# Two accumulating products of a mixer block joined in one PSUM bank, with the hand-written step tables that go with it

## What is computed

```python
x = x + _L0_conv_ref(_gn(x), w_qkv, w_o)            # attention, 12 heads of 16, over 1024 tokens
x = x + _L1_conv_ref(_gn(x), w1, b1, w2, b2, bias_w, bias_b)

# _L1_conv_ref(x, ...)
bias = x @ bias_w.T + bias_b                         # the linear path
xf = jnp.fft.rfftn(xb, axes=(1, 2), norm='ortho')    # over H and W, four blocks of 48 channels
r1, i1 = relu(complex product with w1, + b1)
r2, i2 = second product with w2, + b2
out = jnp.fft.irfftn(complex(r2, i2), s=(H, W), axes=(1, 2), norm='ortho')
return out + bias
```

## Time and profile before

| | |
|---|---|
| median of three runs | 1474.7 us (1470.56 to 1479.0) |
| the profiled execution's own time | 1474.24 us |
| its span on the core | 1472.4 us |
| PE busy | 1414.4 us (96% of the span) |
| DVE, ACT busy | 1156.4 us (79%), 1009.3 us (69%) |
| TensorE clock granted, mean | 0.986 of full speed |

### The profile page before, as it was taken

The page is one execution under the profiler, slowest core; times in us unless marked ns, Lnnn a source line. Parts: engine busy times, 40 slices in busy tenths (PEclk is TensorE's granted clock), DMA queues, the critical chain, the costliest instruction groups (busy, mean ns, idle before and its releaser), DMA issues.

```text
span 1472.4 us, 27421 instructions
## 1 busy us (share of the span) xinstructions
PE 1414.4 (96%) x9984; PEld 682.2 (46%) x9984; DVE 1156.4 (79%) x2155; ACT 1009.3 (69%) x2018; POOL 187.6 (13%) x277
## 2 busy tenths in 40 slices
PE   6999889999999999999999999998999999999978
PEld 4543334545444454544545444544545454434455
DVE  4888888987899879987799878986799878988041
ACT  1267777677767777677767777676776777677812
POOL 2000001030013000040011200040010400040000
PEclk9699999999999999999999999999999999999999
DMA  7400431242430533333430523324322324312213
GB/s 149 78 12 17 95 66 29 44 106 74 84 88 24 121 83 61 69 86 87 94 84 21 127 67 72 74 65 91 88 62 50 82 76 87 88 30 65 64 44 89
DMA packets 100606, 106.37 MB, mean 72 GB/s; under 512 B 24760, under 2 KB 77560, under 8 KB 100472
## 3 DMA queue, kind: packets, MB, share of 16 engines
q1 hardware_dynamic: 98616, 102.80, 30.6%
q10 hardware_dynamic: 1856, 1.82, 0.6%
HBM read 26.99 MB, written 6.67 MB: 23 GB/s over the span
## 4 chain that ended last, share of the span: by engine, by line
PE 85%; DVE 7%; DMA 3%; SPq 2%; issue 1%; ACT 1%; POOL 0%; ACTq 0%; POOLq 0%; DVEq 0%
PE o_acc L1313 24%; PE ring L1289 16%; PE scores L1251 16%; PE ring L1336 10%; DVE row_max L1049 5%; PE ring L1325 3%; PE ring L1449 2%; PE ring L1436 2%; PE ring L1442 2%; PE ring L1355 2%; PE ring L1347 1%; PE ring L1428 1%; DMA rows_b<-rows_a 1%; PE ring L1455 1%; SPq L667 1%
## 5 line engine op out<-in xcount | busy, mean ns | idle before, releaser
L1049 DVE TENSOR_REDUCE row_max<-ring 128x1 f32<-128x512 f32 x1536 | 973.9, 682 | 180.9 <-PE ring L1289 174.6
L938 ACT ACTIVATE probs<-scores 128x512 f32<-128x512 f32 x1536 | 829.0, 600 | 260.6 <-PE scores L1251 259.7
L1289 PE MATMUL ring<-k_stack,q_stack 48*128 48x512 f32 x1536 | 592.5, 463 | 26.2 <-DVE row_max L1049 16.5
L1251 PE MATMUL scores<-q_stack,k_stack 50*128 50x512 f32 x1536 | 594.8, 460 | 1.3 <-ACT probs L938 1.2
L1313 PE MATMUL o_acc<-probs,v_aug 128*18 128x512 f32 x3072 | 405.5, 600 | 2.4 <-ACT probs L938 1.2
L1251 PEld LDWEIGHTS scores<-q_stack,k_stack 50*128 50x128 f32 x1536 | 243.7, 185 | 314.1 <-ACT probs L938 300.2
L1289 PEld LDWEIGHTS ring<-k_stack,q_stack 48*128 48x128 f32 x1536 | 247.6, 187 | 147.4 <-DVE row_max L1049 95.7
L583 POOL TENSOR_TENSOR inv_all<-o_raw,inv_all 128x1024 f32<-128x1024 f32 x23 | 54.5, 2371 | 573.9 <-DMA inv_all<-inv_rows 573.9
L1313 PEld LDWEIGHTS o_acc<-probs,v_aug 128*18 128x18 f32 x3072 | 52.0, 96 | 122.7 <-issue 86.9
L1336 PE MATMUL ring<-xt,w_qk 64*128 64x256 f32 x540 | 67.9, 379 | 1.3 <-DVE xt L1088 1.3
L1336 PEld LDWEIGHTS ring<-xt,w_qk 64*128 64x128 f32 x540 | 53.7, 186 | 11.7 <-DVE row_max L1049 3.8
(11 more groups left out here) (159 smaller groups left out, 1058.5 us busy)
## 6 DMA issues: line engine op xcount, KB each, us to landing
q_stack<-qk_parts SPq DMA_DIRECT2D x288, 64.0 KB, 2.3
k_stack<-qk_parts SPq DMA_DIRECT2D x141, 128.0 KB, 4.1
inv_all<-inv_rows SPq DMA_DIRECT2D x23, 512.0 KB
rows_b<-rows_a SPq DMA_DIRECT2D x122, 96.0 KB, 2.8
x_in<-in_x_dram SPq DMA_DIRECT2D x8, 768.0 KB, 6.4
x_res<-in_x_dram SPq DMA_DIRECT2D x8, 768.0 KB, 5.2
spec_b<-spec_a SPq DMA_DIRECT2D x60, 102.0 KB, 2.5
o_t<-inv_all SPq DMA_DIRECT2D x184, 32.0 KB, 1.9
```

Of the source, the lines that this page charges most:

```text
L938: nc.scalar.activation(probs[:, GH * (s % 2) + h, :], scores[:, n % SCORE_BANKS, :], ACT.Exp, scale=SCALE).then_inc(probs_made, 1)
L1049: nc.vector.tensor_reduce(row_max[:, which, m:m + 1], max_bank(b, g, unit, i), AX.X, ALU.max).then_inc(max_taken, 1)
L1251: mm(scores[:, n % SCORE_BANKS, :], k_stack[rows, 2 * g + hp, P * kt:P * (kt + 1)], q_stack[rows, g, half, hp, :], start=True, stop=True). ...
L1289: mm(max_bank(b, g, unit, i), q_stack[rows, g, half, hp, P * qt:P * (qt + 1)], k_stack[rows, 2 * g + hp, HALF * which:HALF * (which + 1)], ...
```

## The change

"idftw" disappears as a kind. "lin" moves behind the last transform, to steps 51, 53, 55 and 56. Each pair first makes its six 64-row products with the group left open, then adds `iw` times `rows_b` for the same two tiles, one 128-row product of 192 columns into each of the two banks. DVE adds bank and `x1` once, into `tok_n`. The store waits for "lin" 7. In the tail the four late pairs stand where one pair and four "idftw" stood, and all four pairs of the last image stand behind "idfth". The tables change in other places as well.

```diff
-    4: ([('turn', 2)], []),
+    6: ([('turn', 2)], []),
...
-    29: ([('lin', 0)], []),
...
-    36: ([('lin', 1)], []),
-    37: ([('mix1', 2)], []),
-    38: ([('mix1', 3), ('mix1', 4), ('mix1', 5), ('mix1', 6), ('mix1', 7)], []),
+    36: ([('mix1', 2)], []),
+    37: ([('mix1', 3)], []),
+    38: ([('mix1', 4), ('mix1', 5), ('mix1', 6), ('mix1', 7)], []),
...
-    44: ([('lin', 2)], []),
...
-    50: ([('lin', 3)], []),
-    53: ([('idftw', 0)], []),
-    54: ([], [('idftw', 1)]),
-    55: ([('idftw', 2)], [('idftw', 3)])}
+    51: ([('lin', 0)], []),
+    53: ([('lin', 1)], []),
+    55: ([('lin', 2)], []),
+    56: ([('lin', 3)], [])}
...
-PREP_FOLLOW = {0: [('stats', 0)], 3: [('stats', 1)], 6: [('stats', 2)], 7: [('gather', 0)], 12: [('normalise', 0)], 13: [('normalise', 1)], 14: [('normalise', 2)]}
-POST_FOLLOW = {14: [('stats', 0)], 15: [('stats', 1)], 16: [('stats', 2), ('gather', 0)], 26: [('normalise', 0), ('normalise', 1)], 27: [('normalise', 2)]}
-PLACE_V_AT = {26: 2, 40: 0, 45: 1}
-TOKENS_AT = {20: (0,), 21: (1,), 24: (2,), 27: (3,), 28: (4,), 30: (5,)}
-STACK_AT = {10: 'q1', 11: 'q0', 13: 'k'}
+PREP_FOLLOW = {0: [('stats', 0)], 4: [('stats', 1)], 6: [('stats', 2)], 7: [('gather', 0)], 12: [('normalise', 0)], 13: [('normalise', 1)], 14: [('normalise', 2)]}
+POST_FOLLOW = {14: [('stats', 0)], 15: [('stats', 1)], 16: [('stats', 2), ('gather', 0)], 25: [('normalise', 0)], 27: [('normalise', 1)], 33: [('normalise', 2)]}
+PLACE_V_AT = {28: 2, 40: 0, 43: 1}
+TOKENS_AT = {21: (0,), 23: (1,), 25: (2,), 27: (3, 4), 30: (5,)}
+STACK_AT = {9: 'q0', 11: 'q1', 13: 'k'}
...
-SPREAD_AT = 5
+SPREAD_AT = 3
...
-LOAD_AT = 26
+LOAD_AT = 23
```

```diff
-                    nc.vector.tensor_tensor(x1[:, t, :], bank_[:, 0:C], x1[:, t, :],
+                    nc.vector.tensor_tensor(tok_n[:, t, :], bank_[:, 0:C], x1[:, t, :],
                                             ALU.add).then_inc(done, 1)
...
-                if kind == "idftw":
-                    post_taken(dve, b, "lin", 7)
-                    nc.vector.tensor_tensor(tok_n[:, 2 * k:2 * k + 2, :],
...
-            def inverse_part(b, k, bank_):
-
-                if k == 0:
-                    pe.wait_ge(lines_in, 16 * NT * (b + 1))
-                return mm(bank_[:, 0:2 * C], const("iw"), rows_b[:, 2 * k:2 * k + 2, :],
-                          start=True, stop=True)
...
-                    ends = tokens_by(banks, k, xt1, bias_t)
+                    tokens_by(banks, k, xt1, bias_t, False)
+                    if k == 1:
+                        pe.wait_ge(lines_in, 16 * NT * (b + 1))
+                    ends = [mm(banks[half][:, 0:C], const("iw"), rows_b[:, token_tile(k - 1 + half), :],
+                               start=False, stop=True) for half in range(2)]
...
-                    if (kind, k) == ("idftw", 0):
+                    if (kind, k) == ("lin", 0):
                         turn_back()
```

More of the change, by code:

```diff
@@ L628, in build @@
         BUSY_LATE = {"start": 0, ("turn", 2): 1, ("mean", 0): 1, ("var", 0): 2, ("spread", 0): 2,
-                     ("dftw", 3): 3, ("dfth", 5): 2, ("mix2", 4): 6, ("lin", 7): 4}
+                     ("dftw", 3): 3, ("dfth", 5): 2, ("mix2", 4): 6, ("idfth", 3): 4}
         SIGNS_AT = 6
@@ L713, in store @@
             def store(b):
-                post_taken(sp, b, "idftw", 3)
+                post_taken(sp, b, "lin", 7)
                 sp.dma_start(image(out, b), tok_n[:, :, :]).then_inc(stored, 16)
@@ L795, in body @@
                                 regroup_lines(sp, b - back)
-                            if kind == "idftw" and k == 3:
+                            if kind == "lin" and k == 7:
                                 store(b - back)
@@ L808, in tail @@
                 for k in range(4):
-                    post_taken(sp, b, "idftw", k)
-                    sp.dma_start(image(out, b)[:, 2 * k:2 * k + 2, :],
-                                 tok_n[:, 2 * k:2 * k + 2, :]).then_inc(stored, 16)
+                    post_taken(sp, b, "lin", 2 * k + 1)
+                    sp.dma_start(image(out, b)[:, k::NT // 2, :],
+                                 tok_n[:, k::NT // 2, :]).then_inc(stored, 16)
                 sp.wait_ge(stored, 16 * (NB - 1 + 4))
@@ L1114, in post_piece @@
                     if not isinstance(b, int) or b > 0:
-                        post_taken(dve, b - 1, "idftw", 3)
+                        post_taken(dve, b - 1, "lin", 7)
                     nc.vector.tensor_tensor(x1[:, t, :], bank_[:, 0:C], x_res[:, t, :],
@@ L1125, in post_piece @@
                                           bank_[:, 0:1]).then_inc(done, 1)
-                if kind == "idftw":
-                    post_taken(dve, b, "lin", 7)
-                    nc.vector.tensor_tensor(tok_n[:, 2 * k:2 * k + 2, :],
-                                            bank_[:, 0:2 * C].rearrange("p (t n) -> p t n", t=2),
-                                            x1[:, 2 * k:2 * k + 2, :],
-                                            ALU.add).then_inc(done, 1)
             def setup(stage, bank_):
@@ L1328, in turn, with upper_lower @@
                 return last
-            def upper_lower(banks, n, operands):
+            def upper_lower(banks, n, operands, closed=True):
                 out = []
@@ L1335, in upper_lower, with tokens_by @@
                         lhs, rhs = operands(half, slice(ROWS * half, ROWS * (half + 1)), c)
-                        out.append(mm(banks[half][:, 0:n], lhs, rhs, start=(c == 0), stop=(c == 2)))
+                        out.append(mm(banks[half][:, 0:n], lhs, rhs, start=(c == 0),
+                                      stop=(closed and c == 2)))
                 return out[-2:]
-            def tokens_by(banks, k, lhs, rhs):
+            def tokens_by(banks, k, lhs, rhs, closed=True):
                 at = slice(P * (k // 2), P * (k // 2 + 1))
-                return upper_lower(banks, C, lambda half, rows, c: (lhs[rows, c, at], rhs[rows, c, :]))
+                return upper_lower(banks, C, lambda half, rows, c: (lhs[rows, c, at], rhs[rows, c, :]),
+                                   closed)
             def of_groups(bank_, values):
@@ L1462, in post_piece @@
                                   start=False, stop=True)
-                if kind == "idftw":
-                    last = inverse_part(b, k, bank_)
                 last.then_inc(post_made, 1)
```

## The result

| | before | changed |
|---|---|---|
| median of three runs, us | 1474.7 (1470.56 to 1479.0) | 1497.67 (1496.2 to 1500.42) |
| ratio, 95% interval | | 1.0143 (1.0104 to 1.0182) |
| measured once more (26 and 7 runs), us | 1476.76 | 1489.7 (1488.49 to 1495.54) |
| ratio, 95% interval | | 1.0098 (1.0068 to 1.0127) |
| span of the profiled execution, us | 1472.4 | 1495.9 |

The change makes the kernel slower by 1.0 to 1.4%. The prediction was 1477.5 us with a range up to 1486. The table gives the difference between profiled executions by place, measured as distances between ACT's exponentials. The prologue is what lies ahead of the first exponential, the tail what lies behind the last.

What follows compares the result with a forecast made beforehand. PE's piece work and the places of the pieces were taken to set the loop, DVE mostly not. The sum was 1474.24 + 1.7 (loop) + 8.5 (tail) - 6.9 (DMAs) = 1477.5 us, range 1468 to 1486 us.

Steps and rivals of the forecast that it cites:

- The products of a pair: Loop, PE: a joined pair takes 1.97 us, seen as 1.9 to 2.0; products change a middle body by -0.1 us.
- The loop's +0.7 us per middle body: Bodies 2 to 6: products, empty fronts, "mix1" and DVE together add 0.7 us each, 3.5 us for five.
- the empty fronts: Loop steps without a piece at their front: 0.44 us each, four full ones replacing 2.5, +0.7 us per body.
- Body 1: First body without late pieces: three pairs leave, two empty fronts and the "mix1" come, -2.2 us.
- The moved normalisations, POOL's token operations and `place_v`: Loop, DVE and POOL: these cost nothing, hidden by the engines' spare time.
- The DMAs, -6.9 us: Regrouped rows ahead of "dfth" 0: loading x_in earlier removes PE's waits, -6.9 us (0 to -6.9).
- Rival 1: Slow rows stay, made by one late DMA engine, not the x_in load: 6.9 us back, 1484.4 us; chance 0.18.
- The base: Start of the sum: the profiled execution at 1474.24 us, 0.5 us under the median of the runs.
- The tail, +8.5 us: After the loop: image 6 +5.5 us, image 7 +3.0 us, together +8.5 us (7 to 10).
- Rival 2: Late steps: DVE was the bound and its saved additions count, 14 us less, 1463.5 us; chance 0.08.
- Rival 3: Tail: clock falls after a longer wait for `rows_b`, slowing "dfth" by 3.2 us, 1480.7 us; chance 0.13.
- Rival 4: Loop and tail: pairs cost less, 1.81 us each, saving 0.6 us per body and 1.7 in the tail, 1472 us; chance 0.08.

Runs made afterwards that it cites:

- load23: Kernel before with only the load of x_in moved from step 26 to 23, nothing joined: 1471.6 us, ratio 0.9975.
- fill21: load23 with the three early qk pairs spread over steps 17, 19 and 21, leaving one front fewer empty: 1473.77 us, ratio 0.9981.
- bias_late: Changed kernel with POOL's two additions of the bias moved from steps 27 and 30 to step 46: 1487.31 us, ratio 1.0082.
- norm_moved: load23 with the first normalisation of xt1 at step 25 and the others at 27, nothing joined: 1482.63 us, ratio 1.0036.
- norm_back: Changed kernel with the normalisations of xt1 back at steps 26, 26 and 27: 1487.51 us, ratio 1.0073.
- prep_back: Changed kernel with the tables for the image to come (turn 2, its statistics, stacking of q1 and q0) as before: 1491.92 us, ratio 1.0114.
- tail_busy: norm_back with seven instead of three keep_busy products behind "dftw" 3 in the tail: 1486.8 us, ratio 1.0065.
- joined_best: norm_back with the tail's pairs opened ahead of the waits and seven keep_busy products behind "dftw" 3: 1482.11 us, ratio 1.003.
- joined_late: bias_late with the tail's pairs opened ahead of the waits and seven keep_busy products behind "dftw" 3: 1482.76 us, ratio 1.0044.
- after_again: Changed kernel run again word for word for a second profile: 1489.7 us, ratio 1.0098.
- after_busy0: Changed kernel with body 0's third and fourth setup-stage PE work made four times and twice over: 1497.45 us, ratio 1.0125.
- busy0: load23 with body 0's third and fourth setup-stage PE work made four times and twice over: 1473.77 us.

## Why the prediction was wrong, step by step

- **The products of a pair** were right. From a pair's first product to the next tiles the trace shows 1.94 us (1.9 to 2.0 was said), in the steps forecast:

```profile
579.38 1.17 PE L1328 MATMUL ring<-bias_t,xt 64*128 64x192 f32 x12
580.47 0.92 PE L1373 MATMUL ring<-rows_b,cst 128*128 128x192 f32 x4
581.32 0.49 PE L1281 MATMUL ring<-k_stack,q_stack 48*128 48x512 f32 x1
```

- **The loop's +0.7 us per middle body** was right: with the collision out of the way bodies 2 to 6 are 168.9 us, and those of `load23`, unjoined, 168.05: +0.8. The signs of the single rows were as argued, though the empty fronts were sized a little high (`fill21`). Body 1 was put too low: -1.2 us without step 26 against -2.2. The last body was 1.6 us above the +0.4, and 1.0 more came at step 20 in the first profile, where the clock fell for 3.4 us; the second lacks it. In all the loop without step 26 and the late rows is +4.7 us and not +1.7: this term was mis-sized by 3.0.
- **"The moved normalisations, POOL's token operations and `place_v` are costed at nothing: DVE's spare time and POOL's hide them."** This is the step whose mechanism failed: 6.6 us in the first profile, 3.7 in the second. The spare time was there; the two engines got into each other's way, and a reduction that PE was waiting for stood behind. `bias_late` and `norm_moved` show it from both sides. It does not carry the miss alone: `norm_back` and `bias_late`, which are free of it, took 1487.5 and 1487.3 us, still 10 us above the forecast.
- **The DMAs, -6.9 us.** In the two first profiles the term came out (-7.2). As a property of the kernel it was mis-sized: three more profiles of before have 0.6 to 2.5 us of it. Rival 1 had the cause more nearly right (a late DMA of one execution), but not the consequence: its absence takes nothing from the changed kernel's time, it takes the gain from the forecast.
- **The base.** The sum started from an execution with the least fall of the clock in body 0 seen (160.4 us; three others of the same kernel 167.8 to 169.2). Its 6.5 us of late rows happened to bring it to the median, and the forecast took them away while leaving the short body 0 in. With these two put right the sum is 1474.7 + 1.7 + 8.5 - 1.4 = 1483.5 us (1.4 being the mean of the late rows in the three other profiles), and with the loop as measured 1486.5, where `norm_back` and `bias_late` have 1487.5 and 1487.3. The collision (3.7 to 6.6) makes it 1490.2 to 1493.1, where the second measurement has 1489.7. This is an estimate worked out afterwards, within the spread of the executions, and it leaves out the clock in the tail.
- **The tail, +8.5 us.** Measured +9.8: image 6 +5.2 (5.5 forecast), the last pairs +4.2 (4.4; the terms given for it add up to 4.2), the removed pairs -1.1 (-1.4), and 1.5 us of the clock. `prep_back`, the one profile with this tail in which the clock did not fall, has +8.6.
- **Rival 2** (DVE the bound, 14 us) is refuted at its price: no body shrank, and DVE's saved work given back costs 0.7 of its 2.2 us in a body. **Rival 3** came true: behind waits of 3.35 to 4.30 us the "dfth" products of the tail took 5.3 to 6.2 us in eight of nine profiles of joined kernels. But in `prep_back`, behind a wait of 3.65, they took 3.8, and in `fill21`, with nothing joined and the same wait of 2.45 us behind which seven other profiles have 3.8, they took 5.4. So the wait does not decide it alone. Where it was under 1 us (`tail_busy`, `joined_best`, `joined_late`) they took 3.8 each time. Two stretches of the changed kernel's tail at the lower level:

```profile
1437.00:1440.00 3.00, 3.00 (x4) 0.67 (x2) 0.00 (x0) 0.00 (x0) 1.75 (x7) 0.50 0.00 0
1454.00:1457.00 3.00, 3.00 (x15) 2.93 (x14) 0.00 (x0) 1.37 (x3) 0.00 (x0) 0.50 0.00 0
```

The first of them lay among `keep_busy` products of the tail, which were no protection, and so did most of the ten microseconds at the lower level in `after_again`. The falls ahead of "dfth" rival 3 did not have; they make the greater part of the 4.7 us of that tail. **Rival 4** did not come: pairs cost 1.94 us.

What remains open is the clock, in body 0 above all. Body 0 took 160.4 to 169.2 us in four executions of the kernel before, 161.1 and 166.9 in two of the changed one, and 170.3 in `after_busy0`. The first measurement of the changed kernel (1497.67 us) lies 8 us above the second. Between their profiled executions, 8.6 us apart, body 0 makes 5.8, step 26 2.9, the prologue 2.5 and step 20 of body 7 1.0, and the longer tail of the second takes 3.6 back. What decides the fall in an execution was not found. The prologue, from 65.7 to 69.3 us over all profiles, was not taken apart.

## What to carry to other kernels

Work that is moved on an engine with time to spare is not free until the engine beside it is looked at: ask what POOL runs in that microsecond, and whether something that PE waits for stands behind. A term taken from one event in one profile (a single late row, a body that is short) is to be seen in a second execution before it goes into the sum. Joining two accumulations that run alone in their slots saves neither columns nor PE time; here it only bound the hidden product to the late operand, and the tail paid for it (5.2 and 4.2 us at its two places).

## What the hardware showed beyond the expected

- DVE's `TENSOR_SCALAR` on 128x512 float32 takes 0.54 us alone; behind a POOL instruction that began first it ends 0.28 to 0.29 us after that one's end, up to 2.10 us in all (`after_busy0`); 34 such in five profiles.
- The mean granted clock of whole executions on one core was 0.984 in the shortest and 0.975 in the longest execution of one kernel, 1470.59 and 1482.38 us (`busy0`): an estimate of 1.3 us for each 0.001. It does not order them strictly: the execution with 0.986 took 1471.72 us.
